# Two-layer graph network on 2048 nodes: unit 24 turned by DMA instead of TensorE, and sixteen adjacency loads issued from ScalarE

## What is computed

```python
h = jnp.maximum(_layernorm(x, axis=-1), 0.0)
x = x + _L0_gnn_ref(h, adj, L0_gnn_adj_scaling_factor, L0_gnn_weight, ...)   # 4-bit weights and activations:
#   support = relu(quant(h) @ quant(weight)); output = adj @ quant(support)
h = jnp.maximum(_layernorm(x, axis=-1), 0.0)
x = x + _L1_gnn_ref(h, adj, adj)
#   M = (adj + adj.T) * 0.5 + I; d = M.sum(1) ** -0.5; y = (adj @ (d * M * d)) @ h
```

## Time and profile before

| | |
|---|---|
| timed runs, median of 3 | 495.15 us (493.93 to 495.35) |
| profiled execution, its own time | 496.49 us |
| its span, first to last instruction | 494.7 us |
| TensorE matmul busy | 478.1 us (97%) |
| VectorE / ScalarE / GpSimd busy | 268.5 / 154.1 / 46.6 us |
| DMA engines, mean busy share from 38 to 138 us | 1.03 |

### The profile page before, as it was taken

One profiled execution on the slowest core, in us unless ns is written; L12 is line 12 of the kernel. 1 busy time (PEld: TensorE's weight loads), 2 busy tenths in 40 slices (PEclk: granted clock), 3 DMA queues, 4 the chain that ended last, 5 costly groups with the idle time before them and its releaser, 6 DMA issues.

```text
span 494.7 us, 6414 instructions
## 1 busy us (share of the span) xinstructions
PE 478.1 (97%) x2358; PEld 232.0 (47%) x2358; DVE 268.5 (54%) x360; ACT 154.1 (31%) x300; POOL 46.6 (9%) x54
## 2 busy tenths in 40 slices
PE   1899999999999999999999999999999999999997
PEld 1755544444454444444444444444444444444446
DVE  4966996779999688876997767340100001000010
ACT  1787833767562435344521121140000000000000
POOL 2320963213200000000000000000000000000000
PEclk9999999999999999999999999999999999999999
DMA  8986999999986242332232321045010000100001
GB/s 286 401 333 161 233 193 231 225 220 229 233 241 249 65 135 98 95 117 85 85 122 91 113 99 42 0 168 193 23 42 21 21 21 21 42 21 21 21 23 43
DMA packets 63180, 62.66 MB, mean 127 GB/s; under 512 B 46136, under 2 KB 46392, under 8 KB 63160
## 3 DMA queue, kind: packets, MB, share of 16 engines
q1 hardware_dynamic: 63152, 62.40, 44.3%
q10 hardware_dynamic: 8, 0.00, 0.0%
HBM read 42.99 MB, written 8.39 MB: 104 GB/s over the span
## 4 chain that ended last, share of the span: by engine, by line
PE 84%; DVE 8%; DMA 4%; SPq 2%; ACT 1%; issue 1%; POOL 0%; ACTq 0%
PE ps_a L1204 31%; PE ps_p L1102 13%; PE ps_p L1167 7%; PE ps_a L1167 7%; PE ps_b L1167 7%; PE ps_m L1167 4%; PE ps_h L1167 4%; DMA feat<-in_x 2%; PE ps_b L1053 1%; PE ps_m L1102 1%; PE ps_h L1102 1%; DVE at L763 1%; DVE small L944 1%; PE ps_b L1220 1%; PE ps_a L1220 1%; PE ps_a L1053 1%
## 5 line engine op out<-in xcount | busy, mean ns | idle before, releaser
L1102 PE MATMUL ps_p<-small,at 128*128 128x512 f16 x448 | 99.2, 379 | 0.4 <-DVE feat L884 0.4
L1022 DVE SCALAR_TENSOR_TENSOR feat<-ps_a,feat 128x512 f32<-128x512 f32 (+1 forms) x16 | 10.8, 675 | 148.7 <-PE ps_a L1204 144.2
L1204 PE MATMUL ps_a<-small,at 128*128 128x512 f16 x360 | 80.2, 379 | 0.0
L1204 PE MATMUL ps_a<-a_in,at 128*128 128x512 f16 x360 | 80.2, 379 | 0.0
L1102 PEld LDWEIGHTS ps_p<-small,at 128*128 128x128 f16 x448 | 43.7, 98 | 50.8 <-DVE feat L884 0.7
L584 ACT ACTIVATE split<-a_in 128x1024 f16<-128x1024 f32 x30 | 31.7, 1057 | 101.8 <-PE ps_p L1167 90.0
L940 DVE TENSOR_TENSOR split<-a_in,split 128x1024 f16<-128x1024 f32 x30 | 36.7, 1224 | 34.0 <-ACT split L584 34.0
L1204 PEld LDWEIGHTS ps_a<-small,at 128*128 (+1 forms) x360 | 35.2, 98 | 42.5
L1204 PEld LDWEIGHTS ps_a<-a_in,at 128*128 (+1 forms) x360 | 35.2, 98 | 42.5
L1167 PE MATMUL ps_p<-feat,split 128*128 (+1 forms) x180 | 43.9, 379 | 0.5 <-DVE small L944 0.5
L1167 PE MATMUL ps_a<-feat,split 128*128 (+1 forms) x180 | 43.8, 379 | 0.0
(11 more groups left out here) (182 smaller groups left out, 436.0 us busy)
## 6 DMA issues: line engine op xcount, KB each, us to landing
a_in<-in_adj SPq DMA_DIRECT2D x46, 512.0 KB, 3.9
at<-in_adj SPq DMA_DIRECT2D x16, 512.0 KB, 8.9
out<-feat SPq DMA_DIRECT2D x31, 256.0 KB, 4.3
feat<-in_x SPq DMA_DIRECT2D x8, 512.0 KB, 11.6
feat<-out SPq DMA_DIRECT2D x4, 1024.0 KB, 9.3
at<-in_L_gnn_weight SPq DMA_DIRECT2D x2, 512.0 KB, 4.0
at<-at SPq DMA_TRANSPOSE x42, 4.7
split<-in_adj SPq DMA_DIRECT2D x1, 512.0 KB, 15.7
```

The source lines that it names most:

```text
L1022: nc.vector.scalar_tensor_tensor(out, products, 1.0 / (SA * SZ), out, ALU.mult, ALU.add).then_inc(y_out, 1)
L1102: last = nc.tensor.matmul(l0_bank(r), at_block(r, lo, j), small[:, j * D:(j + 1) * D], start=(j == 0 and lo == 0), stop=(j == T - 1 and lo ...
L1204: last = nc.tensor.matmul(BANK[n], at_block(t, lo, j), z_part(j, z_lo), start=(j == 0 and lo + z_lo == 0), stop=(j == T - 1 and lo == 1))
```

## The change

Unit 24 goes from `TURNED` to `MOVED`: its 8 transposes on TensorE, its pass from PSUM on ScalarE, its row sum pass and its two VectorE passes go; one `hi_rows`, one `lo_rows` and two DMA transposes come, in round 9 between moves 23 and 25. The loads of units 16 to 31 are issued by ScalarE on its own queue, each just behind a `hi_rows`, with the waits of `free_slot` now on ScalarE's sequencer; SP keeps the transposes. The column sums of units 10 and 14 go from ScalarE (four half passes) to VectorE (`column_sum_late`, in rounds 5 and 7), and ScalarE gets those of unit 24. The last column sums stand one round earlier. One small VectorE operation is added after round 13.

```diff
-EVEN = (10, 12, 14, 18, 20, 22, 26)
-SUMMED = EVEN
+EVEN = (10, 12, 14, 18, 20, 22, 24, 26)
+SUMMED_LATE = (10, 14)
...
         MOVES = {1: [9], 2: [10, 11], 3: [12], 4: [13, 14], 5: [15], 6: [17, 18], 7: [19, 20], 8: [21, 22],
-                 9: [23, 25], 10: [26], 11: [27, 29]}
+                 9: [23, 24, 25], 10: [26], 11: [27, 29]}
...
-        SUMS_OF = {5: [[(10, FIRST)], [], [(10, LAST)]], 7: [[(12, FIRST)], [(12, LAST)], []],
-                   8: [[(14, FIRST)], [(14, LAST)], []], 9: [[(18, FIRST)], [(18, LAST)], []],
-                   10: [[], [], [(20, FIRST)]], 11: [[], [(20, LAST)], [(22, FIRST)]],
-                   12: [[], [], [(22, LAST), (26, FIRST)]], 13: [[], [], [(26, LAST)]]}
+        SUMS_OF = {7: [[(12, FIRST)], [(12, LAST)], []], 8: [[(18, FIRST)], [(18, LAST)], []],
+                   9: [[(20, FIRST)], [(20, LAST)], []], 10: [[(22, FIRST)], [], [(22, LAST)]],
+                   11: [[], [], [(24, FIRST), (24, LAST)]], 12: [[], [], [(26, FIRST), (26, LAST)]]}
...
+        LOADS = {9: [16], 10: [17], 11: [18], 12: [19], 13: [20], 14: [21], 15: [22], 17: [23], 21: [24], 22: [25],
+                 23: [26], 24: [27], 25: [28], 26: [29], 27: [30], 29: [31]}
...
-            LOADS = {9: [16], 10: [17], 11: [18], 12: [19], 13: [20], 14: [21], 15: [22], 17: [23], 20: [24], 21: [25], 22: [26],
-                     23: [27], 25: [29, 28], 26: [30], 27: [31]}
             for r in range(1, 12):
                 for u in MOVES[r]:
                     move(u)
-                    for w in LOADS.get(u, []):
-                        if w < AHEAD:
-                            rows(w)
-                        else:
-                            rows_again(w)
...
+            def load_behind(u):
+                for w in LOADS.get(u, []):
+                    if w >= AHEAD:
+                        free_slot(act, before(w))
+                    rows(act, w)
...
                 for u in moves[1:]:
                     hi_rows(u)
+                    load_behind(u)
...
+                for k, u in enumerate(SUMMED_LATE):
+                    if r == (5, 7)[k]:
+                        wait_moved(dve, u)
+                        column_sum_late(u)
```

More of the change, by code:

```diff
@@ L306, in arrivals, with rows, free_slot @@
             return 16 if u < AHEAD else 16 * ((u - AHEAD) // RING + 2)
+        def rows(engine, u):
+            engine.dma_start(unit_in(u), adj[(u // 2) * P:(u // 2 + 1) * P, (u % 2) * W:(u % 2 + 1) * W])\
+                  .then_inc(arr_sem(u), 16)
+        def free_slot(engine, u):
+            if u in ADDED:
+                engine.wait_ge(acc_done, ADDED.index(u) + 1)
+            if u in MOVED:
+                engine.wait_ge(lo_ready, MOVED.index(u) + 1)
+            else:
+                engine.wait_ge(turned, turn_no(u) + 1)
+                engine.wait_ge(rs_done, TURNED.index(u) + 1)
         @block.sync
@@ L311, in load_x @@
                 sp.dma_start(feat3[:, 2 * n:2 * n + 2, :], x_tiles[:, 2 * n:2 * n + 2, :]).then_inc(x_in[n], 16)
-            def rows(u):
-                sp.dma_start(unit_in(u), adj[(u // 2) * P:(u // 2 + 1) * P, (u % 2) * W:(u % 2 + 1) * W])\
-                  .then_inc(arr_sem(u), 16)
-            def rows_again(u):
-                free_slot(before(u))
-                rows(u)
-            def free_slot(u):
-                if u in ADDED:
-                    sp.wait_ge(acc_done, ADDED.index(u) + 1)
-                if u in MOVED:
-                    sp.wait_ge(lo_ready, MOVED.index(u) + 1)
-                else:
-                    sp.wait_ge(turned, turn_no(u) + 1)
-                    sp.wait_ge(rs_done, TURNED.index(u) + 1)
             def move(u):
@@ L337, in move @@
                     elif u >= 12:
-                        free_slot(waited_in(u)[lo])
+                        free_slot(sp, waited_in(u)[lo])
                     sp.dma_start_transpose(at_half(u // 2, lo, u % 2).rearrange("p (b i) -> p b i", i=P), stage(u, lo))\
@@ L354, in _ @@
                 load_x(n)
-            rows(0)
-            rows(1)
+            rows(sp, 0)
+            rows(sp, 1)
             for n in range(2, T // 2):
@@ L359, in _ @@
             for u in range(2, 12):
-                rows(u)
+                rows(sp, u)
             sums(0)
@@ L363, in _ @@
             sp.wait_ge(hT_ps, T // 2)
-            rows(12)
-            rows(13)
+            rows(sp, 12)
+            rows(sp, 13)
             move(3)
@@ L368, in _ @@
             sp.wait_ge(sq_ready, T // 2)
-            rows(14)
-            rows(15)
+            rows(sp, 14)
+            rows(sp, 15)
             move(7)
-            LOADS = {9: [16], 10: [17], 11: [18], 12: [19], 13: [20], 14: [21], 15: [22], 17: [23], 20: [24], 21: [25], 22: [26],
-                     23: [27], 25: [29, 28], 26: [30], 27: [31]}
             for r in range(1, 12):
@@ L971, in _ @@
             link(nc.vector.memset(pause[:, :], 0.0))
+            late_sums = colp[:, :].rearrange("p (u b) -> p u b", b=B)[:, SUMMED_LATE[0]:SUMMED_LATE[-1] + 1:4, :]
+            nc.vector.tensor_scalar(late_sums, late_sums, 1.0 / SA, None, ALU.mult)
             link(nc.vector.tensor_scalar(colp[:, a:b], colp[:, a:b], 1.0 / SA, None, ALU.mult))
```

5 lines of the change are left out of this document (2 added, 3 removed).

## The result

The changed kernel took **507.19 us** in the median of 6 runs (503.13 to 510.25), the kernel before 495.24 us on the same chip (6 runs, 493.93 to 495.35). The ratio is 1.024 (95% interval 1.021 to 1.027). The prediction was 492.7 us, with a range of 491.8 to 495.8 us: the sign was wrong, and the time lies far outside of the range.

A forecast was written before the change was run, and what follows sets the result against it. TensorE, busy 478.1 of 494.7 us, was taken to bound the kernel, so only its work and waits count. Gains 0.87 + 0.61 + 1.02 = 2.50 us took 495.15 to 492.65 us, range 491.8 to 495.8.

The forecast's parts named there:

- Part 1: Unit 24's turn of 8 transposes leaves TensorE, all of it on the path: 0.87 us, called certain.
- Part 2: TensorE's wait at 128.11 us for VectorE's x1_tile(10) goes, as 2.24 us of VectorE work leave round 10: 0.61 us.
- Part 3: TensorE's wait before turn(30) at 136.92 us goes, as unit 27's transposes land earlier: 1.02 us.
- X: Landing time of unit 27's transpose, 133.18 us before; taken as 129 to 130; 130.67 needed for the whole gain.
- more fitting end: Later bound of unit 27's landing, 133.5 us, allowing for SP's queue standing still from 127.7 to 130.1 us.
- high end: Unit 27 lands at 135.9 us: loads at 1.7 us as now, two added transposes 2.7 us, no gap to fill.
- Part 4: Sixteen load issues on ScalarE, 0.53 us each, finish before turn(28) is done: no cost.
- the third rival: ScalarE's loads each stand behind a transpose's issue, near 2.4 us; gain 0.8 us, 494.4 us; chance 0.10.
- 107.9 + 12.7 + 5p: When ScalarE reaches hi_turned(28), with five load issues of p each: 123.3 us at p = 0.53; break at 2.0 us.
- Part 5: Two late column sums on VectorE, ScalarE's changed passes and the added small operation behind round 13: 0.
- The sum, 2.50 us: Total gain from the turn and TensorE's two waits: 0.87 + 0.61 + 1.02 us, from 495.15 to 492.65 us.
- The second: Rival: two added transposes on a full DMA stream land unit 27 at 135.9, loss 2.7 us, 497.9 us; chance 0.10.

The follow-up runs named there:

- experiment 1: Changed kernel with all loads back on SP between the moves, unit 24 still moved: 497.36 us, ratio 1.006 to the kernel before.
- Experiment 9: Changed kernel with all loads back on SP and the 12 loads of units 20 to 31 cut to 64 KB: 492.94 us, ratio 0.995.
- experiment 10: Kernel before, unit 24 still turned, with the 12 loads of units 20 to 31 on SP cut to 64 KB: 493.74 us, ratio 0.997.
- experiment 5: Changed kernel with all loads back on SP, load 28 behind move 24 and load 29 behind move 25: 498.3 us, ratio 1.007.
- experiment 3: Changed kernel with the 12 loads of units 20 to 31 on ScalarE's queue cut from 512 to 64 KB: 498.78 us, ratio 1.010.
- 12: Changed kernel with the 12 loads of units 20 to 31 cut to 64 KB and unit 31's load behind sum_hi(1): 496.96 us, ratio 1.002.
- experiment 8: Kernel before with the loads of units 2 to 5 issued by ScalarE at the start, no transpose in flight: 500.99 us in one run.
- 7: Changed kernel with 12 loads on ScalarE's queue in 7 pieces of 512 bytes a line, 448 of 512 KB each: 502.45 us, ratio 1.016.
- 11: Kernel before, unit 24 turned, with the loads from unit 16 on issued by GpSimd behind its adds: 503.80, 509.78, 511.84 and 514.85 us.
- experiment 2: Kernel before, unit 24 turned, with the loads from unit 16 on issued by ScalarE: 507.03 us, ratio 1.022.

## Why the prediction was wrong, step by step

**What bounds the kernel: right.** TensorE and its waits decide. `layer0` waited for no transpose in the trace before, but the trace doesn't say by how much the transposes were early. In one queue the reserve was enough for two more of them (experiment 1); for transposes that take up to 12 us it was not.

**Part 1, 0.87 us, right.** 8 transposes less, 192 products in a row; 9 against 10 gives 0.87 us in the stage. "This is certain" held for the work and not for the time, since TensorE is saved nothing if it waits later.

**Part 2, 0.61 us: the wait went, the reason was at best a part.** It also goes with unit 24 still turned, when only the stream is shorter (experiment 10). VectorE was late because the units came late. In the changed kernel a wait of the same kind, 0.51 us, stands one round earlier, at 127.87 us.

**Part 3, the second wait: here the prediction failed.** The step is "I take X = 129 to 130, nearer to the low end, since the loads now leave SP's queue while the transposes issue, as in the row of four transposes." The row of four transposes in the earlier trace rows shows transposes with nothing beside them. After the change the loads are still there, on another queue, and in the same DMA traffic. The bounds had the same gap: both ends, 1.3 and 1.7 us for a load, were prices in one queue, and I had no row at all for a load beside a transpose on another. Measured, the stream falls from 210 to 171 GB/s, a transpose's median landing goes from 4.8 to 6.0 us and at worst to 12. In the changed kernel the second transpose of unit 27, the one ahead of `hi_turned(28)`, was issued at 138.81 us and landed at 144.87. That is X, 15 us behind my value. The rest of the part held. In experiment 1, with unit 24 alone, the same transpose lands at 133.50 us in a trace whose `turn(16)` starts 1.26 us earlier, so X is 134.76 in the time of the trace before: between the "more fitting end" of 133.5 and the high end of 135.9. The formula "the gain is 133.18 - X" then gives -1.58 us, and the stage got 1.58 us longer; the 3.74 us from the landing to `turn(30)` came out as 3.74 and 3.73. So the chain and its price were right and the landing was mis-sized, by some 5 us for unit 24 in one queue and by the rest of the 15 for the second queue. Arrivals that I hadn't followed were late too (units 28 and 29 in experiments 1 and 5); they decide only once the landing of unit 27 doesn't, in experiment 5.

**Part 4, ScalarE's loads: the issue right, the wait forgotten.** An issue costs 0.33 to 0.39 us, below the 0.53 that I took; none came near 2 us. (That a full queue holds an issue for 2.4 us at most was misread: one transpose's issue took 3.73 us in the trace before. It changes nothing here.) The Trainium skill, "Perfetto Trace Analysis", section "DMA Instruction — HWDGE (DVE, Sync)", lists a lock wait; it didn't show on ScalarE's issues, so the third rival, in the form in which I wrote it, is refuted. But my 107.9 + 12.7 + 5p has only what ScalarE executes. A load also waits for its slot, and all of ScalarE's order waits with it: 5.56 us at the load of unit 31 in experiment 3, and 3.0 us of its stage (3 against 12). In the changed kernel this doesn't decide, since there the transpose ahead of `hi_turned(28)` lands later still.

**Part 5, priced at 0: not tested by itself.** Experiment 9 has both late column sums and the added small operation, and its stage comes out at the sum within 0.04 us, so they cost nothing there.

**The sum, 2.50 us: right under a condition that this kernel doesn't meet.** In the changed kernel itself 16.8 us of new losses stand against it.

**The rivals.** The second, "the moves end later", had the right mechanism for unit 24 (0.10, 497.9 us; experiment 1 gave 497.4), and by the transfer that it named. That its number is so near is in part luck: it put the loss at 2.7 us, and the stage lost 1.6. None had the cause of the other 10 us. It also was the rule that I weighed: the Trainium skill, "DMA: Bandwidth & Descriptors", section "Issuing engines are not separate DMA queues", says that DMAs of any engine interleave on the same 16 DMA engines and that spreading the issue saves only the sequencer's time. By that the loads gain nothing, and experiment 8 agrees for plain loads (417 against 396 GB/s while both queues are at work). Beside transposes the measurement goes further than the rule: the second queue costs 10 us with unit 24 moved and 12 without. I had set the trace's 4.4 us a move against the rule as a sign of slack, and there was none to be had this way.

**The range** took in the bounds of terms that I had, and none for "a combination that no row shows". Had a quarter of the chance been put there, the range would have had to reach above 500.

**What stays open:** why transposes and plain loads disturb each other across queues. Bytes in flight matter (3), the length of the pieces perhaps somewhat (7), the issuing engine does not (11). Whether it is the way an engine changes between its queues or the transposing hardware itself, no run here tells. Every run with a second queue also starts loads beside transposes that are still in flight; one in which each load waits for their landing would tell the queue from the moment of the load, and none was made. Transposes on ScalarE's queue and loads on SP's weren't tried. Open too are some 4 us in the median between experiments 12 and 9, in runs that left no trace. No version beat the kernel before with all of its data.

## What to carry to other kernels

Where DMA transposes and large loads are in flight together, try one queue first, in the order in which they are wanted; here a second queue that cost its issuer next to nothing slowed both. When the DMA share is at one, take an added transfer at its full price in the queue, and follow the transfers behind it to whoever wants them: the one that decides can change (experiments 1 and 5). And where a change brings two kinds of traffic together as no row of the trace does, measure that alone first, or widen the range on that side.

## What the runs showed of the hardware

- Loads of 512 KB on a second queue beside DMA transposes: the DMA share rises (1.06 to 1.14, 1.19 in experiment 2) while the rate falls (210 to 171 and 166 GB/s). In one stretch of 8 us it is 100 GB/s at a share of 1.14, and a packet of the transposing queue takes 83 ns on average, against 21 ns with transposes alone. A high share is thus no sign of a high rate.
- Two queues of plain loads (one trace, 12 to 16 us): 417 GB/s against 396 in one queue: no loss.
- Transposes with 64 KB loads land in 3.3 us in the median, with 512 KB loads on the same queue in 4.8, with them on another queue in 6.0 (ScalarE's) and 6.1 (GpSimd's), all from 60 to 130 us. From 60 to 84 us alone it is 4.7 in one queue, and 8.8 and 12.4 beside the second.
- A DMA issue of 512 KB took 0.33 to 0.39 us on ScalarE in all 16 issues, against 0.53 us in the median on SP.
- The waits cost more than their length: behind idle times of 4.1 and 5.0 us the granted clock of the stretch was 0.91 and 0.92, and matmuls took 4.2 us more than at 1.00. Right behind them it was 0.61 (97.6 to 102 us) and 0.50 (148.6 to 150.3). Not every wait had this: 2.46 us in experiment 1 left it at 1.00, 2.23 us in experiment 5 was followed by 0.78.
